# Two taps per convolution product, and another order of the pieces in the half slots, in a Mamba, mixture-of-experts and linear-attention kernel

## The reference, cut to what matters

```
x = hidden                                   # [8, 512, 256]
xn = layernorm(x)
x_in, z = split(xn @ W_in.T)                 # 512 channels each
def branch(x_in, z):                         # once forward, once over reversed time
    xc = silu(conv(x_in, conv_w) + conv_b)   # one filter of 4 taps per channel, over time
    dt, B, C = split(xc @ Wx.T)              # 64, 16, 16
    dt = softplus(dt @ Wdt.T + bdt)          # [512 positions, 512 channels]
    # a state of 16 numbers per channel:
    h[t] = exp(dt[t] * A) * h[t-1] + dt[t] * B[t] * xc[t]
    y[t] = sum over the 16 states of h[t] * C[t]
    return (y + xc * D) * silu(z)
s = (branch forward + branch backward) / 2 @ W_out.T
g = silu(mixture_of_experts(xn))             # 8 experts, 2 for each position
x = x + s * g
```

## Time and profile before

| what | us |
|---|---|
| median of 3 runs (3226.63 to 3227.58) | 3227.04 |
| the profiled execution, its time | 3248.7 |
| its span, first to last instruction | 3246.9 |
| one loop turn (a batch), 696.78 to 948.93 | 252.15 |

### The profile page before, as it was taken

How to read it: one execution, slowest core, us unless ns; L and a number is a source line. 1 busy time by engine, 2 the same in 40 slices (tenths; PEclk the granted TensorE clock), 3 DMA queues, 4 the chain that set the end, 5 groups by cost and what they waited for, 6 DMA issues and landing times. The chain is left out here.

```text
span 3246.9 us, 40447 instructions
## 1 busy us (share of the span) xinstructions
PE 2737.8 (84%) x13486; PEld 1826.9 (56%) x13486; DVE 2252.4 (69%) x2812; ACT 1765.3 (54%) x2691; POOL 1754.2 (54%) x554
## 2 busy tenths in 40 slices
PE   5466887887888888878968878777999999999999
PEld 5134665665666565666656656555455555555554
DVE  5287989889889989989988988984442442442430
ACT  1355767758848758758758767641332332322322
POOL 0598868878878878778778887861000000000000
PEclk9777898899999989989989989887999999999999
DMA  6222324333333334333333332323000000000000
GB/s 254 85 69 94 119 101 140 108 109 119 123 106 121 107 104 147 109 105 117 129 115 115 111 134 90 130 89 131 26 33 0 32 32 0 32 18 15 6 7 7
DMA packets 149278, 283.24 MB, mean 87 GB/s; under 512 B 23659, under 2 KB 97878, under 8 KB 149078
## 3 DMA queue, kind: packets, MB, share of 16 engines
q1 hardware_dynamic: 142934, 264.08, 23.8%
q0 software_dynamic: 6144, 16.79, 1.5%
HBM read 239.13 MB, written 41.68 MB: 86 GB/s over the span
## 5 line engine op out<-in xcount | busy, mean ns | idle before, releaser
L708 POOL TENSOR_TENSOR hs<-u,bb 128x2048 f32<-128x2048 f32 x256 | 1159.3, 4534 | 368.5 <-PE hT L1013 323.3
L884 DVE TENSOR_TENSOR_SCAN hs<-dA,hs 128x1024 f32<-128x1024 f32 x512 | 1166.3, 2284 | 122.7 <-POOL hs L708 75.9
L797 ACT ACTIVATE dA<-dt,cols 128x511 f32<-128x511 f32 x1024 | 661.8, 680 | 412.9 <-DVE hs L884 408.6
L1013 PE MATMUL hT<-ident,hs 128*128 128x128 f32 x3584 | 558.4, 297 | 264.2 <-DVE held L894 222.4
L1013 PEld LDWEIGHTS hT<-ident,hs 128*128 128x128 f32 x3584 | 434.9, 151 | 405.6 <-DVE held L894 290.2
L894 DVE SCALAR_TENSOR_TENSOR held<-hT,ct,held 128x512 f32<-128x512 f32 x864 | 603.8, 742 | 54.2 <-PE hT L1013 53.1
L1287 ACT ACTIVATE gl<-bank,cols_sb 128x512 f32<-128x512 f32 x192 | 130.7, 687 | 528.4 <-PE bank L1526 528.1
L1526 PE MATMUL bank<-mT,cms_sb 128*128 128x512 f32 x768 | 363.6, 598 | 10.1 <-ACT mT L1281 8.6
L1032 PE MATMUL moe<-xgT,held 128*128 128x128 f32 x2400 | 334.4, 299 | 30.0 <-ACT xgT L811 28.2
L1032 PEld LDWEIGHTS moe<-xgT,held 128*128 128x128 f32 x2400 | 321.3, 214 | 61.4 <-ACT xgT L811 37.6
L136 POOL COPY cur<-slot 128x8 uint32 (+1 forms) x8 | 1.5, 187 | 640.9 <-DVE held L148 631.3
(11 more groups left out here) (219 smaller groups left out, 3332.1 us busy)
## 6 DMA issues: line engine op xcount, KB each, us to landing
held<-wl SPq DMA_DIRECT2D x75, 1024.0 KB
bb<-b_scratch SPq DMA_DIRECT2D x128, 512.0 KB, 5.6
held<-wl SPq DMA_DIRECT2D x75, 512.0 KB
xg_scratch<-zero SPq DMA_DIRECT2D x10, 960.0 KB, 5.4
xg<-xg_scratch SPq DMA_DIRECT2D x75, 128.0 KB
yg_scratch<-yg SPq DMA_DIRECT2D x75, 128.0 KB, 1.7
held<-x SPq DMA_DIRECT2D x16, 512.0 KB, 8.7
cb<-b_scratch SPq DMA_DIRECT2D x32, 256.0 KB, 4.7
```

The lines of the kernel that those rows point to most:

```text
L708: nc.gpsimd.tensor_tensor(hs[n % HS][:, :, :], u[d][:, :, :], row, ALU.mult).then_inc(dBu_ready, 1)
L797: last = nc.scalar.activation(dst, src, ACT.Exp, scale=cols[:, at:at + 1])
L884: nc.vector.tensor_tensor_scan(h, decay, h, 0.0, ALU.mult, ALU.add).then_inc(scan_done, 1)
L1013: last = nc.tensor.transpose(hT[c % 2][:, k * P:(k + 1) * P], hs[n % HS][:, k, c * P:(c + 1) * P], ident[:, :])
```

## The change

Three things change together.

**The convolution takes two taps per product.** ACT copies each proj result in two halves of 64 partitions, channels 0 to 63 into `xpad[0]` and 64 to 127 into `xpad[1]`. Two transfers per block, issued by SP (`shift`), copy each half into the other 64 partitions of its tile, one position earlier. A product over 128 partitions with a 128 x 64 stationary operand then sums two taps of 64 channels. A conv is still four products of 512 columns, but each writes 64 output partitions, g = 0 the lower and g = 1 the upper ones. PE waits for the transfers before each conv of d = 0 (`shifted[k]`). At the start, the diagonals are made by 64 DVE instructions of 64 x 64 in place of 32 of 128 x 128, and four small loads are added.

**The tables.** While d = 1 runs, proj moves from half slots 0, 1, 6, 7 to 0, 1, 5, 6; conv from 2, 4, 8, 10 to 2, 4, 9, 10; dt from 13, 14, 16, 17 to 14, 17, 19, 21; soft on ACT from 17 to 21; c from 21 to 22. While d = 0 runs, soft moves from 15 to 16 and c from 16 to 17. The five tiles start at 0, 6, 12, 19, 26 (d = 0) and 0, 6, 12, 18, 25 (d = 1), before at 0, 6, 12, 18, 24 in both. SKIP goes from 0, 1, 4, 5 to 0, 3, 4, 5. POOL's four soft instructions, before after state 13, 14, and 15 (two), now come after 13, 14, 14, 15 (d = 0) and 14, 14, 15, 15 (d = 1).

**Late decays.** In the half slots of `LATE`, ACT does the decay after preparation and tile pieces, not before.

```diff
                 sp.dma_start(cols[:, :], cols0).then_inc(w_sem, 16)
+                for g in range(2):
+                    for half in range(2):
+                        sp.dma_start(w_tap[HP * half:HP * (half + 1), g, :], cols0[HP * g:HP * (g + 1), CW:CB]).then_inc(w_sem, 16)
...
-            plan(0, "proj", (0, 1, 6, 7))
-            plan(0, "conv", (2, 4, 8, 10))
+            plan(0, "proj", (0, 1, 5, 6))
+            plan(0, "conv", (2, 4, 9, 10))
...
-            plan(0, "dt", (13, 14, 16, 17))
-            plan(0, "soft", (17,))
+            plan(0, "dt", (14, 17, 19, 21))
+            plan(0, "soft", (21,))
...
-            SKIP = (0, 1, 4, 5)
+            SKIP = (0, 3, 4, 5)
+
+            SOFT = ((13, 14, 14, 15), (14, 14, 15, 15))
+
+            LATE = ((6, 7, 9, 18, 23, 30), (0, 3, 4, 8, 9, 18, 21, 22, 23, 25, 29, 30))
...
+            def pair_at(d, q):
+
+                return 2 * q if d == 0 else 2 * (KC - 1) - 1 - 2 * q
...
+            TILE_AT = ((0, 6, 12, 19, 26), (0, 6, 12, 18, 25))
...
+                def shift(k, unit):
+
+                    sp.wait_ge(p_used, use_of("proj", k, 0, unit) + 1)
+                    for g in range(2):
+                        own, other = slice(HP * g, HP * (g + 1)), slice(HP * (1 - g), HP * (2 - g))
+                        sp.dma_start(xpad[g][other, k, KC - 2:KC - 2 + L], xpad[g][own, k, KC - 1:KC - 1 + L]).then_inc(shifted[k], 16)
...
                         for n in range(NS):
+                            if d == 1 and more:
+                                for what, k in PREP[0][2 * n] + PREP[0][2 * n + 1]:
+                                    if what == "proj":
+                                        shift(k, unit + 1)
...
                     if what == "proj":
-                        nc.scalar.activation(xpad[:, k, KC - 1:KC - 1 + L], src[:, :], ACT.Copy).then_inc(p_used, 1)
+                        for g in range(2):
+                            own = slice(HP * g, HP * (g + 1))
+                            last = nc.scalar.activation(xpad[g][own, k, KC - 1:KC - 1 + L], src[own, :], ACT.Copy)
+                        last.then_inc(p_used, 1)
...
-                        for t in range(KC):
-                            at = t if d == 0 else 2 * (KC - 1) - t
-                            last = mm(dst[:, :], taps[:, (d * DB + k) * KC + t, :], xpad[:, k, at:at + L], start=(t == 0), stop=(t == KC - 1))
+                        if d == 0:
+                            pe.wait_ge(shifted[k], 32 * (b + 1))
+                        for q in range(KC // 2):
+                            at = pair_at(d, q)
+                            for g in range(2):
+                                last = mm(dst[HP * g:HP * (g + 1), :], taps[:, d, k, g, q, :], xpad[g][:, k, at:at + L],
+                                          start=(q == 0), stop=(q == KC // 2 - 1))
```

More of the change, by code:

```diff
@@ L436, in bass_mamba_moe_then_linear_attention_mlp @@
             xnT = s0("xnT", [P, KD, L])
-            xpad = s0("xpad", [P, DB, L + 2 * (KC - 1)])
+            xpad = [s0(f"xpad{g}", [P, DB, L + 2 * (KC - 1)]) for g in range(2)]
             zs = s0("zs", [P, DB, L])
@@ L594, in _ @@
                     sp.sem_inc(q, 16)
+                for k in range(DB):
+                    shift(k, 0)
                 store_b(0, 0)
@@ L827, in body @@
                                 s = 2 * n + j
-                                if n + 3 < NS:
-                                    decay(d, unit, n + 3, j)
-                                elif more:
-                                    decay(1 - d, unit + 1, n + 3 - NS, j)
+                                if s not in LATE[d]:
+                                    if n + 3 < NS:
+                                        decay(d, unit, n + 3, j)
+                                    elif more:
+                                        decay(1 - d, unit + 1, n + 3 - NS, j)
                                 if more:
@@ L836, in body @@
                                     tile(piece, b, i)
+                                if s in LATE[d]:
+                                    if n + 3 < NS:
+                                        decay(d, unit, n + 3, j)
+                                    elif more:
+                                        decay(1 - d, unit + 1, n + 3 - NS, j)
                                 if s in SKIP:
@@ L922, in body @@
                                     scan(1 - d, unit + 1, n + 2 - NS, j)
-                                if n == 0 and d == 0 and later(b):
-                                    for k in (2 * j, 2 * j + 1):
+                                for k in range(DB) if d == 0 and later(b) else ():
+                                    if FIN[k] == 2 * n + j:
                                         finish(b - 1, k)
```

52 lines of the change are left out of this document (33 added, 19 removed).

## The result

| kernel | median us | ratio to before, 95% interval |
|---|---|---|
| before | 3227.04 | |
| the change | 3245.65 (3243.53 to 3249.26) | 1.0061 (1.0046 to 1.0076) |

The change is 0.6% slower. Forecast were 3205 and, with 0.76, faster; the time lies above the range. The profiled execution of the change took 3249.26 us (its span 3247.5). That of before stood 21.7 us above its own median, and 13.8 us of its difference to a second profile of the kernel before (span 3223.0) lie ahead of the first weighing; so its start can't be set beside this one. In the scan loop the two profiles of before agree within 0.2 us.

The account below looks back on a forecast made before the run. DVE was taken to bound the scan stage, with POOL's list limiting what its idle time gives back. Terms 0.7 + 1.8 + 1.0 + 0.7 - 0.5 - 0.5 = 3.2 us a turn, x 7 = 22, gave 3205 us; 8-in-10 range 3176 to 3233.

Parts of the forecast that it names:

- the start: Before the loop: -6.8 us for four shorter convs, +5 for transfers and copies, +1.5 for 64 small DVE instructions; counted as nothing.
- the transfer for k = 0: First conv of d = 0 waits for its transfer behind a tile's load: 0.5 us lost a turn, bounds 0 and 3.9.
- the rival: Transfer for k = 0 lands late, each microsecond past 822.7 costing DVE one; at 828, 3238 us; chance 0.14.
- The column halves overlap, 1.9: Convolution on PE: a product of four takes 1.9 us instead of 3.60, the two column halves running side by side.
- The rule that I named for the rival: Skill rule cited for column halves not overlapping in the convolution: gain 7 us, 3220; chance 0.14.
- Its worth on the path, 0.7 a turn: Shorter convs free 13.6 us of PE work a turn, of which DVE gains only 0.7.
- 0.7 - 0.5 - 0.5: Per turn: convolution gain 0.7 us, less 0.5 for ACT's added copies, less 0.5 for waiting on the k = 0 transfer.
- The order tables: Per-turn gains: soft and dt later in d = 1, 0.7 us; tile 4 and soft in d = 0, 1.8; B pair earlier, 1.0.
- POOL's list bounds: From state 11 to the next unit's state 0, POOL's gapless work lets only 0.7 us (d = 1) and 1.8 (d = 0) through.
- POOL's list is no bound: State 11 comes earlier, so the middle gaps pay in full: 9.5 x 7 = 66 us, 3161; chance 0.2.
- The rival of the late decays: A late decay sits on DVE's path in d = 1, 1 us at four half slots: 3230 us; chance 0.04.
- the bounds of the two waits: Bounds per turn: 0 and 1.2 us for ACT's copies, 0 and 3.9 for the k = 0 transfer; giving 3190 to 3219.

Follow-up runs that it names:

- wide_order: The change with diagonals in 8 broadcast multiplications, transfers of k = 0 and 1 and the B pair issued before the held-back tile store and load: 3205.14 us.
- taps_wide: The change with all diagonals built by 8 broadcast DVE multiplications of 64x512 instead of 64 of 64x64: 3229.64 us, ratio 1.0007.
- wide_old: Two-tap product, diagonals in 8 broadcast multiplications, tables of before except projections of k = 2 and 3 one half slot earlier: 3226.20 us, ratio 1.0001.
- wide_tile24: The change with diagonals in 8 broadcast multiplications and the last tile of d = 0 back at half slot 24 from 26: 3207.09 us, ratio 0.9942.
- shift_first: The change with only the k = 0 transfers issued ahead of the store and load of the tile ending at half slot 31: 3257.90 us, ratio 1.0097.

## Why the prediction was wrong

Two terms of the sum failed, the start and the transfer for k = 0. Put right (wide_order), they give back 40.5 us.

**"The start ... I count nothing": some 16 us.** The step was "64 small DVE instructions for 32, an estimated +1.5". They took 20.28 us, 13.7 more than the 32. I had priced the small one below the large one; per instruction it is half as long again. The clearing of the whole `xpad` ahead of them, another 4 us, had no term. The -6.8 for the convs is there in taps_wide (3.65 and 3.67 us for two, before 7.03), but in the change itself the lower clock behind the long wait took it back (6.59 and 6.61). The wait for a transfer was 3.40.

**The transfer for k = 0, "I take 0.5" a turn: the largest miss, and it was the rival.** Forecast were 3.5 us in all, with bounds of 0 and 3.9 a turn. The change of the queue's order gives 24.5, for six waits; that is 4.1 each, the upper bound (by the profiles 3.2: d = 1 is +2.9 in taps_wide and -0.3 in wide_order). The place, the queue, the load in front and the turn behind were named. The choice inside the bounds failed: I took the transfer to land soon after the load's bytes (820.5 to 822.5), by a rate of 323 GB/s. The row of the B pair, 5.6 us behind the same load, was the nearer one: issued at 820.68, the transfers had landed when the conv began at 826.20, 5.5 later. The rival had 0.14.

Its way was not quite the rival's either. The prediction's times are those of the first profile of before, where the unit began 1.66 us earlier (795.95, here 797.61). In that time the conv began at 824.5, 1.8 past the 822.7 from which each microsecond was to count. The conv took 0.8 us longer than its 1.94 and the turn 0.9 longer than its 1.04 at the lower clock, for which I had no term. 1.8 + 0.8 + 0.9 = 3.5, and that is by how much this ninth scan is late: 33.9 us (831.50 - 797.61) behind the first one, before 30.4. By this sum about half of the loss in this turn is the late start of the conv, the other half the clock behind it.

**"The column halves overlap, 1.9": right.** 1.94 us, and 125.4 us in all for 480 records of PE, in the second profile of before 218.8. The rule that I named for the rival (the Trainium skill, TensorE: Matmul & The Clock Gate, Part 3: Packing small matmuls) speaks of weight loads, which are to overlap running products only where the row groups differ. It doesn't hold here: in the conv at 832.51 the weight load at 833.00 stands inside products that use the same 128 rows, and so does one before the change (821.37, in the conv at 820.93). Nor does a conv cost anything at its edges: 799.30 + 1.94 = 801.24, and the next turn starts at 801.16. The drain that a change of the tiling mode is to bring (the Trainium skill, TensorEngine Tiling (Array Packing), Key Properties) isn't to be seen in these rows, which leave no gap for it.

**Its worth on the path, 0.7 a turn: not told apart.** wide_old has the product, its copies and its transfers with the tables of before. By the forecast's terms that is 0.7 - 0.5 - 0.5 = -0.3 a turn; measured is no difference, within 0.1% or some 0.4 a turn. Its ninth scan comes 0.4 us earlier than before, and by the end of the unit nothing is left of that; both are too small to read a gain or a loss from.

**The order tables: right in mechanism, and they depend on the product.** In d = 0, 1.8 was forecast and 2.4 measured. In d = 1, 1.4 with everything; wide_order has 0.3, wide_tile24 1.3. POOL's list bounds, as forecast: in wide_order the second scan of n = 12 comes 5.7 us earlier than before, the next one, n = 13, only 1.1. That excludes the rival "POOL's list is no bound", and the sign for it, DVE idle for POOL hs in the middle of d = 1, is there (4.65 and 4.46). What I missed is that the list begins when the first half of the unit lets it: state 11 stood 3.7 us back in the change, so what the first half loses passes to the end. And I had no thought that the tables could lose by themselves, as they do with the long product; that step is open. The rival of the late decays isn't what happened: without them the change is slower, and DVE waits 0.30 for a decay in the middle of d = 1, where it waited 3.82. Late decays do keep DVE waiting with the long product (2.1 us in the first 20 scans of d = 1), but four of them put back made that kernel no faster.

**The sum.** 3205 was forecast. wide_order, the change with its two defects taken out, has 3205.1. The change is 40.5 us above it: 16.0 for the diagonals, 24.5 for the queue's order. That the two agree so closely is partly luck: d = 1 gives less than forecast, d = 0 more. Of the signs, the one for being wrong was there, PE idle 3 us and more before the conv of k = 0, released by a transfer; the turn of 249 was not (252.46), and came with wide_order (249.63).

Three figures of the prediction don't follow from its own terms. With the bounds of the two waits (0 and 1.2, 0 and 3.9) the sum runs from 3198 to 3233, not from 3190 to 3219. In the first rival, 3183 is half way from 3205 to 3161; half of its 66 us gives 3194. And 1 us at four decays in 7 turns, set on 3205, is 3233, not 3230. None of this would have reached 3245.65.

## What to carry to other kernels

Where a new transfer goes into a queue, list what is issued ahead of it and behind it; behind a load of a megabyte and more, price it by what else lands there, not by its own bytes. Moving one transfer ahead only passed the wait on here: move the load, and keep all the small ones together. And to the price of a wait add what the engine loses in clock behind it. Count instructions at the start as well, and price a new shape of instruction by a measured row, not by its elements.

## What the runs showed of the hardware

- 64 DVE instructions of 64x64 took 317 ns each, back to back, where 31 of 128x128 took 206. In 8 instructions of 64x512, 706 ns each, the same work takes 5.65 us. Why the small ones are slower each wasn't tried.
- Two halves of 64 stationary columns, each with all 128 rows, run at the same time: 16 records (two convs) in 3.65 us at the start, 7.03 with full ones.
- Waits for a transfer in the loop cost TensorE more than themselves: the granted clock of the next 5 us was 0.64 in the change (826 to 831 us) and 0.50 in shift_first (829 to 833), and 1.00 in wide_order at the same work. Behind all six waits of the change (2.69 to 4.23 us) the conv took 2.63 to 3.68 us in place of 1.94. It isn't so behind each wait: after 3.16 us at the start of taps_wide (107 us) the clock was 1.00.
- A transfer of 128 KB within the core lands 2.2 us behind its issue at best, up to 2.9 in the loop where no load stands ahead of it (k = 0 and 1 of wide_order). Right behind a tile's load it took 4.0 to 7.6 (k = 0 of the change) and 6.0 to 8.4 (k = 3).
- One kernel's profile can stand 22 us above its median: the two profiles of before differ by 24 us, 13.8 of them ahead of the first weighing (175.74 and 161.90).
